# Three edits to a six-layer fp32 kernel: paired values rounds, moved output weights, more split slices

## What is computed

```python
# MoE: 16 experts, 4 chosen per token, inner width 256, plus one shared expert
scores = sigmoid(x @ gate_w.T) + bias
topk_w, topk_idx = top_k(scores, 4); topk_w /= sum(topk_w)
z   = silu(x @ Wg[e].T) * (x @ Wu[e].T)          # for the experts of the token
out = sum_e topk_w[e] * (z @ Wd[e].T)            # + the shared expert
# causal attention: 32 query heads of 16, 8 key/value groups
scores = q @ k.T / 16;  probs = softmax(where(causal, scores, min))
ctx    = probs @ v
out    = ctx @ w_dense.T + b_dense
```

## Time and profile before

| | |
|---|---|
| time, median of 3 runs | 1367.78 us (1367.69 to 1369.11) |
| the profiled execution, whole | 1367.37 us |
| its span in the profile | 1365.6 us |
| PE busy | 1144.0 us (84%) |
| DVE busy | 837.1 us (61%) |
| ACT busy | 665.5 us (49%) |
| POOL busy | 537.6 us (39%) |
| routed blocks of the first and second MoE layer | about 86 to 326 us, and to 1085 us for the second |
| causal core | 439 to 724 us |
| output projection | 725 to 765 us |

### The profile page before, as it was taken

One profiled execution on the slowest core, in us unless ns is written; L12 is line 12 of the kernel. 1 busy time (PEld: TensorE's weight loads), 2 busy tenths in 40 slices (PEclk: granted clock), 3 DMA queues, 4 the chain that ended last, 5 costly groups with the idle time before them and its releaser, 6 DMA issues. The chain is left out here.

```text
span 1365.6 us, 22222 instructions
## 1 busy us (share of the span) xinstructions
PE 1144.0 (84%) x5800; PEld 723.2 (53%) x5801; DVE 837.1 (61%) x1527; ACT 665.5 (49%) x1218; POOL 537.6 (39%) x578
## 2 busy tenths in 40 slices
PE   5979999996284899999985796999999808777687
PEld 4747677674173344444424584676776605465454
DVE  4857777773455787777722565777777524445542
ACT  3136666663232277777772222666666503334133
POOL 4325555553673233333324324455555442050130
PEclk9979999998587699999998797999999957979879
DMA  9256989555405440000001454689955550010001
GB/s 349 100 203 156 241 238 248 100 104 90 183 35 133 95 89 2 1 1 1 1 1 39 181 189 170 179 206 264 253 107 100 81 167 0 4 37 0 20 12 62
DMA packets 63497, 151.64 MB, mean 111 GB/s; under 512 B 12560, under 2 KB 17488, under 8 KB 58832
## 3 DMA queue, kind: packets, MB, share of 16 engines
q1 hardware_dynamic: 40224, 99.83, 21.4%
q0 software_dynamic: 22592, 50.27, 19.4%
q10 hardware_dynamic: 624, 0.85, 0.4%
HBM read 105.75 MB, written 44.97 MB: 110 GB/s over the span
## 5 line engine op out<-in xcount | busy, mean ns | idle before, releaser
L715 POOL DMA_INDIRECT moe_acc_rows<-moe_out_rows,moe_token_of x94 | 165.4, 1760 | 196.5 <-ACT moe_out_rows L790 190.4
L1782 DVE TENSOR_REDUCE causal_top<-causal_mx 128x1 f32<-128x512 f32 (+3 forms) x384 | 192.0, 550 | 58.6 <-PE causal_mx L1634 50.5
L1746 ACT ACTIVATE causal_prob<-causal_sc 128x512 f32<-128x512 f32 (+3 forms) x384 | 169.9, 492 | 73.2 <-PE causal_sc L1652 70.7
L819 DVE TENSOR_TENSOR moe_w_lo<-moe_raw,moe_w_hi 128x1024 fp32r<-128x1024 f32 x94 | 115.1, 1225 | 112.7 <-ACT moe_w_hi L778 99.6
L730 PE MATMUL moe_gu<-moe_raw,moe_xt_plain 128*128 x376 | 180.5, 603 | 2.4 <-ACT moe_w_hi L778 2.4
L1631 PE MATMUL causal_mx<-causal_ks,causal_qs 96*128 (+4 forms) x384 | 130.9, 351 | 19.2 <-DMA causal_qs<-causal_parts 15.7
L778 ACT CAST moe_w_hi<-moe_raw 128x1024 fp32r x94 | 98.2, 1045 | 95.2 <-issue 90.8
L1652 PE MATMUL causal_sc<-causal_qs,causal_ks 99*128 (+3 forms) x384 | 123.7, 333 | 2.3 <-ACT causal_prob L1746 1.7
L708 POOL DMA_INDIRECT moe_rows<-moe_xn_rows,moe_token_of x94 | 93.3, 992 | 75.2 <-DVE moe_z L828 31.8
L822 DVE TENSOR_TENSOR moe_down_lo<-moe_raw,moe_down_hi 128x1024 fp32r<-128x1024 f32 x94 | 114.5, 1218 | 0.0
L735 PE MATMUL moe_gu<-moe_w_hi,xt_hi 128*128 128x512 f32 x188 | 112.7, 600 | 0.0
(11 more groups left out here) (273 smaller groups left out, 2425.0 us busy)
## 6 DMA issues: line engine op xcount, KB each, us to landing
moe_raw<-in_w_gu SPq DMA_DIRECT2D x34, 1024.0 KB
moe_raw<-in_w_down SPq DMA_DIRECT2D x34, 512.0 KB
causal_qs<-causal_parts SPq DMA_DIRECT2D x42, 128.0 KB, 3.3
moe_acc_rows<-moe_zeros SPq DMA_DIRECT2D x2, 2304.0 KB, 15.2
moe_acc_rows<-x SPq DMA_DIRECT2D x18, 256.0 KB, 2.0
moe_xn_rows<-xn SPq DMA_DIRECT2D x2, 2048.0 KB, 10.9
x<-moe_acc_rows SPq DMA_DIRECT2D x16, 256.0 KB, 5.3
xn<-moe_acc_rows SPq DMA_DIRECT2D x16, 256.0 KB, 5.9
```

The costliest lines, as they stand in the source:

```text
L715: pool.indirect_dma_start(acc_rows[a], bass.IndirectOffsetOnAxis(ap=token_of[:, b - 3:b - 2].bitcast(U32), axis=0), out_rows[(b - 3) % OUT ...
L819: nc.vector.tensor_tensor(w_lo[1 - s][:, :, :], raw[:, bass.ds(at + SPLIT_AT, GU_COLS - SPLIT_AT)].rearrange("p (k n) -> p k n", k=SPLIT), ...
L1746: nc.scalar.activation(prob[u % 2][:, h, o:CH], sc[(u * QPK + h) % BANKS][:, o:CH], ACT.Exp, scale=SCALE).then_inc(exp_done, 1)
L1782: nc.vector.tensor_reduce(top[:, kc, t, h:h + 1], mx[i % BANKS][:, 0:w], AX.X, ALU.max).then_inc(mx_read, 1)
```

## The change

Five edits in three places.

1. `RING` goes from 4 to 8 and gathers are issued 6 blocks ahead (`AHEAD`) rather than 3; the loop bodies of all engines become eight steps long. The copy out goes into the four tiles of `m.xn`, which is free at that time, rather than into buffers of its own.
2. `PLAIN` goes from 2 to 1, so three slices of four are split.
3. The causal core has three `prob` buffers, and TensorE makes values(u-2) and values(u-1) together in each even round, none in odd ones. ACT's wait before a round is one round looser.
4. The output weights come in two halves of 512 KB, loaded by SP during the core. POOL makes `wd_hi`, `wd_lo` of one slice (128x512 each) and adds the bias to one tile of x once a group, behind the select of round 7.
5. In the output projection TensorE makes one tile's transposes, then the product of the tile before, in turn; DVE finishes tile t-2 between them.

```diff
-RING = 4
+RING = 8
+AHEAD = 6
-PLAIN = 2
+PLAIN = 1
...
-            for b in range(-3, NB + 3):
-                if there(b + 3):
-                    if b > 0:
-                        pool.wait_ge(z_done, b)
-                    pool.indirect_dma_start(rows[(b + 3) % RING][:, :], ...
+            for b in range(-AHEAD, NB + 3):
+                n = b + AHEAD
+                if there(n):
+                    if n >= RING:
+                        pool.wait_ge(z_done, n - RING + 1)
+                    pool.indirect_dma_start(rows[n % RING][:, :], ...
...
-            prob = [sb(f"prob{s}", [P, QPK, CH]) for s in range(2)]
+            PROBS = 3
+            prob = [sb(f"prob{s}", [P, QPK, CH]) for s in range(PROBS)]
...
+                    sp.dma_start(wd_raw[:, :, :], m.dram["w_dense"][:, 0:KT // 2, :]).then_inc(dense_in, 16)
+                    sp.dma_start(b_out[:, :], m.dram["b_dense"].rearrange("(a h) -> a h", a=1).broadcast_to([P, H])).then_inc(dense_in, 16)
                     with sp.Fori(1, KV) as g:
                         sp.wait_ge(stack_in, g * (16 * LOADS) - 16 * LOADS // 2)
                         load(g)
+                    sp.wait_ge(wd_ready, KT // 2)
+                    sp.dma_start(wd_raw[:, :, :], m.dram["w_dense"][:, KT // 2:KT, :]).then_inc(dense_in, 16)
...
+                    def prepare_dense(g):
+
+                        if g == 0:
+                            pool.wait_ge(dense_in, 32)
+                        if g == KT // 2:
+                            pool.wait_ge(dense_in, 48)
+                        if g < KT:
+                            raw = wd_raw[:, g % (KT // 2), :]
+                            nc.gpsimd.tensor_copy(wd_hi[:, g, :], raw).then_inc(wd_half, 1)
+                            pool.wait_ge(wd_half, g + 1)
+                            nc.gpsimd.tensor_tensor(wd_lo[:, g, :], raw, wd_hi[:, g, :].bitcast(F32),
+                                                    ALU.subtract).then_inc(wd_ready, 1)
+                        nc.gpsimd.tensor_tensor(m.x[:, g, :], m.x[:, g, :], b_out[:, :], ALU.add).then_inc(x_biased, 1)
...
+                            if u == C0 + 3:
+                                prepare_dense(g)
...
-                                if h == 2 and u >= 1:
+                                if h == 2 and u % 2 == 0 and u >= 2:
+                                    values(g, u - 2)
                                     values(g, u - 1)
-                                elif h == 2 and not first:
+                                elif h == 2 and u == 0 and not first:
+                                    values(g - 1, NS - 2)
                                     values(g - 1, NS - 1)
...
-                            if some(g * NS + u):
-                                act.wait_ge(pv_done, g * NS + u)
+                            if some(g * NS + u - 1):
+                                act.wait_ge(pv_done, g * NS + u - 1)
...
-                    for t in range(T):
-                        transpose_tile(m, pe, cm, xp[t % 2], t, ready=False)
-                    pe.wait_ge(wd_ready, 1)
-                    for t in range(T):
-                        pe.wait_ge(cm.xt_lo, t + 1)
-                        if t >= 2:
-                            pe.wait_ge(x_done, t - 1)
...
+                    pe.wait_ge(wd_ready, KT)
+                    for t in range(T + 1):
+                        if t < T:
+                            transpose_tile(m, pe, cm, xp[t % 2], t, ready=False)
+                        if t >= 1:
+                            pe.wait_ge(cm.xt_lo, t)
+                            if t >= 3:
+                                pe.wait_ge(x_done, t - 2)
...
-                    act.wait_ge(wd_in, 32)
-                    nc.scalar.copy(wd_hi[:, :, :], wd_raw[:, :, :]).then_inc(wd_half, 1)
...
+                    dve.wait_ge(x_biased, T)
+                    for t in range(T):
+                        lo_tile(m, dve, cm, xp[t % 2], t)
+                        if t >= 2:
+                            finish(t - 2)
+                    finish(T - 2)
+                    finish(T - 1)
```

More of the change, by code:

```diff
@@ L627, in routed_blocks @@
         rows = [sb(f"rows{s}", [P, ROW]) for s in range(RING)]
-        out_rows = [sb(f"out_rows{s}", [P, H]) for s in range(OUTS)]
+        out_rows = [m.xn[:, s, :] for s in range(OUTS)]
         xt_plain = [sb(f"xt_plain{s}", [P, PLAIN, P]) for s in range(2)]
@@ L789, in step @@
                         act.wait_ge(scattered[a], (b - 1 - OUTS - a) * 8 + scattered_start[a])
-                    nc.scalar.copy(out_rows[(c - 3) % OUTS][:, :], y[1 - s][:, :]).then_inc(y_out, 1)
+                    nc.scalar.copy(out_rows[(c - 3) % OUTS], y[1 - s][:, :]).then_inc(y_out, 1)
                 if there(b):
@@ L1479, in pb @@
                 return ctx.enter_context(nc.psum_tensor(f"{name}_{what}", shape, dt))
+            wd_hi = outer.enter_context(nc.sbuf_tensor(f"{name}_wd_hi", [P, KT, H], F32R))
+            wd_lo = outer.enter_context(nc.sbuf_tensor(f"{name}_wd_lo", [P, KT, H], F32R))
             BANKS = 3
@@ L1488, in causal_attention_layer @@
             ident = sb("ident", [P, P], BF16)
+            wd_raw = sb("wd_raw", [P, KT // 2, H])
+            b_out = sb("b_out", [P, H])
             warm = sb("warm", [1, 1])
@@ L1720, in _ @@
                     group(KV - 1, False, False)
+                    values(KV - 1, NS - 2)
                     values(KV - 1, NS - 1)
@@ L1856, in _ @@
                 @block.tensor
                 def _(pe):
-                    for t in range(T):
-                        transpose_tile(m, pe, cm, xp[t % 2], t, ready=False)
-                    pe.wait_ge(wd_ready, 1)
-                    for t in range(T):
-                        pe.wait_ge(cm.xt_lo, t + 1)
-                        if t >= 2:
-                            pe.wait_ge(x_done, t - 1)
-                        rows = slice(t * P, (t + 1) * P)
-                        product(nc, yp[t % 2][:, :], [(m.xt_hi[:, k, rows], m.xt_lo[:, k, rows], wd_hi[:, k, :], wd_lo[:, k, :])
-                                                      for k in range(KT)]).then_inc(y_done, 1)
+                    pe.wait_ge(wd_ready, KT)
@@ new lines, in _ @@
+                    for t in range(T + 1):
[5 more added lines that the diff above has]
+                                pe.wait_ge(x_done, t - 2)
+                            rows = slice((t - 1) * P, t * P)
+                            product(nc, yp[(t - 1) % 2][:, :], [(m.xt_hi[:, k, rows], m.xt_lo[:, k, rows], wd_hi[:, k, :],
+                                                                 wd_lo[:, k, :]) for k in range(KT)]).then_inc(y_done, 1)
@@ L1869, in _ @@
                 @block.scalar
                 def _(act):
-                    for t in range(2):
-                        hi_tile(m, act, cm, xp[t % 2], t)
-                    act.wait_ge(wd_in, 32)
-                    nc.scalar.copy(wd_hi[:, :, :], wd_raw[:, :, :]).then_inc(wd_half, 1)
-                    for t in range(2, T):
+                    for t in range(T):
                         hi_tile(m, act, cm, xp[t % 2], t)
@@ L1879, in _, with finish @@
                 def _(dve):
-                    for t in range(T):
-                        lo_tile(m, dve, cm, xp[t % 2], t)
-                    dve.wait_ge(x_biased, 1)
-                    for t in range(T):
+                    def finish(t):
                         dve.wait_ge(y_done, t + 1)
```

31 lines of the change are left out of this document (8 added, 23 removed).

## The result

The changed kernel takes 1353.64 us (1352.23 to 1354.13, four runs), 0.9892 of the kernel before, 95% interval 0.9875 to 0.9909. That is faster by 14 us, and 22 us slower than forecast; it lies above the forecast's range, between B's price (1347) and that of A and B together (1359). B didn't come; A's mechanism did, and cost more than A's price. The profiled execution took 1353.47 us, span 1351.7.

A forecast was written before the change was run, and what follows sets the result against it. TensorE was taken to bound routed blocks and, only just, the core; in the projection waits count. 1367.4 - 15 (slices) - 12 (pairs) + 1.5 (loads) - 10.3 (projection) = 1331.6, median 1332 us; range 1325 to 1340.

The forecast's parts named there:

- B: Routed blocks: rival that ACT binds and a block stays at 5.15 us; 1347 us, chance 0.12.
- A: Core: rival that ACT and DVE lose in a pair what TensorE gains; 1344 us, chance 0.13.
- Split slices: Routed blocks: TensorE saves 0.17 us a block over 94 blocks; taken as -15 us, between 0 and -16.
- C: Routed blocks: rival that DVE's idle time before `w_lo` is a floor, block 5.70 us; 1399 us, chance 0.04.
- TensorE waits for none in the steady part, so 0: Routed blocks: eight gather buffers gain 0, or up to 1 us at the start of each layer.
- Rival D: Routed blocks: DVE and POOL shut each other out, a block takes 5.8 us; 1405 us, chance 0.02.
- The pairs: Core: paired values rounds save 0.19 us a pair, 9.1 in all; with fewer select waits, -12 us together.
- The two signs named for a wrong prediction: Routed blocks: DVE shows no idle time; core: POOL's selects come late in rounds 7 to 9.
- The last group: Core, group without maxima: pairs stop TensorE's waits for the select; -3 us counted for those waits.
- POOL's work in the core: Core: POOL's added operations are hidden between the selects of rounds 7 and 9; without that cover 18 us.
- SP's loads: Core start: two new loads, 768 KB, run beside ACT's loads of the first queries; +1.5 us.
- The projection: Output projection: interleaved transposes and products, no waits for weights or bias; -10.3 us, between -8 and -12.

The follow-up runs named there:

- experiment 12: Kernel before with one plain slice instead of two and its four gather buffers kept: ratio 0.9976.
- Experiments 1 and 2: First: changed kernel with values rounds single again, 1344.7 us (0.9815). Second: kernel before with the pairs and third prob buffer alone, 1.0026.
- 5 to 7: Changed kernel, half the columns for ACT's exponentials, DVE's maxima, or both; one profiled execution each: 32.3, 32.0 and 30.7 us a core group.
- experiment 6: Changed kernel with DVE's maxima over half of each tile's columns; one profiled execution: 32.0 us a core group, last group 25.85 us.
- experiment 1: Changed kernel with its values rounds one at a time again, the other four edits kept: 1344.7 us, ratio 0.9815.
- experiment 9: Changed kernel with single values rounds two behind and output-weight loads behind group 1's: 0.9742; in five rounds 0.9749, against 0.9762 without the move.

## Why the prediction was right and wrong

**Split slices: size right, reason half right.** A block every 4.98 us, ACT's idle time 0.00, no floor under DVE (0.70 us before `w_lo`): near what was worked out (0.53 us for the last), and B and C fell. What failed is the line "TensorE waits for none in the steady part, so 0" for the buffers. It was true of blocks of 5.15 us with a scatter of 1.76, and the edit beside it changes both. Without the buffers 13 of the 16 us are lost (experiment 12), as TensorE then waits 31 us more for gathered rows. I costed two edits one by one against the trace of before, and they are only worth something together.

**Rival D was dismissed on the wrong row.** "`w_lo` takes 1224 to 1226 ns whatever POOL does" shows that DVE isn't held. It says nothing of POOL, which is. The row that tells stood in the earlier trace rows: the scatter at 1745, 1755 and 2259 ns. The Trainium skill (SBUF — State Buffer, Who interferes with whom) has the rule that a DVE instruction with two SBUF inputs contends with a GpSimd instruction that reads SBUF, and that the order of issue decides which one is blocked; the scatters agree: 1.76 us with 0.30 beside `down_lo`, 2.29 with 0.84, and `w_lo` 1.76 to 1.79 in all 40 of the window. The same section infers that such a subtraction doesn't hold up a DMA's descriptors. For this scatter the measurement says otherwise, and it decides. In the changed kernel none of it reaches the time, as TensorE is busy 200.00 of 200 us there behind eight buffers.

**The pairs: the saving right, the balance wrong.** Per pair 0.24 us against 0.19. The step that failed is "DVE has 178 us of work in 236, so there is room". A share over a stage says nothing of eight scores and eight maxima in a row with three banks each. A group was to lose 1.1 us and grew by 1.0: the pairs save 1.4, so by difference the waits grow by 2.5 us a group. Experiments 1 and 2 show that the pairs do it, 5 to 7 that both ACT and DVE are late. Rival A had the mechanism and 0.13 of the chance, but its price, nothing gained, was no bound. Of the 22 us between forecast and result 15 lie in groups 0 to 6. The two signs named for a wrong prediction (no idle time of DVE in the blocks, late selects) didn't come; A's sign, more waits for exponentials and maxima, did.

**The last group: sign right, size not, then lost to the clock.** It was to lose 4.1 us (1.1 for the pairs, 3 for the waits for selects); the pairs alone took 2.3 off (28.1 to 25.8). The changed kernel took 28.7 with two dips of the clock, in both profiles; experiment 6, with the same instructions there and no dip, 25.85. That a dip sets in is seen; what sets it stays open.

**POOL's work in the core** was right: 0 (experiment 1). **SP's loads** were near: +1.5 forecast, +1.4 in the table, 2.2 to 2.4 in experiment 9. **The projection** was right to 0.5 us. **The full attention** cost 2.3 us that nothing in the forecast had; the granted clock was 0.82 in it against 0.84 before, and the cause is open.

## What to carry over

Before grouping work on the bound engine, count how many results the others must take between two such groups and how many buffers hold them; a busy share over the stage can't tell. If a third buffer is to be had, first try it for distance: single rounds two behind were 1.1 to 1.6% faster than the pairs here (with ACT's copy moved by a round). Cost edits that are made together on the trace that the others leave, not on the trace of before.

## What I had not expected of the hardware

POOL's indirect scatter is held up by a DVE subtraction with both inputs in SBUF that is under way when it starts: 1.46 us plus the overlap, and DVE isn't slowed. A subtraction that starts later counts less or not at all: in the changed kernel 71 of 94 gathers have one starting inside them and take 0.94 to 1.00 us as ever (rows 162.35 and 162.67: gather 0.99, `w_lo` 1.76), and two scatters took 2.32 and 1.65 with all of `down_lo` inside.

The granted clock can stand at 0.50 for some 3.4 us where TensorE is busy 4.0 to 4.8 of 5 us on both sides: it did so twice in the last group in both profiles of the changed kernel, once in three of seven profiles with single rounds, not at all in the pairs alone.
